# A graph kernel's list writes moved to other places, its boundary tables built earlier, and a skip product spread over a group

## The reference

```python
edge_index = stack([src, dst])
x = layernorm(x + L0(x, edge_index, ...))              # five attention convolutions
x = layernorm(x + L1(x, edge_index, edge_type, W, attn))   # relation layer, 4 relations
x = layernorm(x + L2(x, edge_index, W1, b1, W2, b2))   # two normalised graph convolutions, elu between
x = layernorm(x + L3(x, src, dst, edge_weight, weight, bias))

def conv(x):            # one of L0's five
    q, k, v = x @ Wq + bq, x @ Wk + bk, x @ Wv + bv    # 4 heads of 32
    alpha = sum(q[dst] * k[src], -1) / sqrt(32)
    attn = softmax of alpha over the edges of one destination
    return segment_sum(v[src] * attn, dst) + x @ Ws + bs
    # then h = gelu(layernorm(conv(h))) + h, the fifth only gelu

def L3(x, row, col, val, weight, bias):                # here the roles are swapped:
    out = segment_sum(val * (x @ weight)[col], row)    # it sums by the edge's source
    return leaky(out + bias)
```

## Time and profile before

| | |
|---|---|
| median of 3 runs | 5692.46 us (5691.0 to 5696.89) |
| the profiled execution | 5703.85 us; span from the first to the last instruction 5702.0 us |
| TensorE, matmuls | 64% busy, mean granted clock 0.689 |
| VectorE | 59% busy |
| ScalarE | 27% busy |
| GpSimd | 71% busy, 4168 instructions |
| DMA | 681.11 MB, mean 119 GB/s |

### The profile page before, as it was taken

The page is one execution under the profiler, slowest core; times in us unless marked ns, Lnnn a source line. Parts: engine busy times, 40 slices in busy tenths (PEclk is TensorE's granted clock), DMA queues, the critical chain, the costliest instruction groups (busy, mean ns, idle before and its releaser), DMA issues. The chain is left out here.

```text
span 5702.0 us, 84663 instructions
## 1 busy us (share of the span) xinstructions
PE 3639.0 (64%) x17936; PEld 2902.4 (51%) x17937; DVE 3386.0 (59%) x9194; ACT 1523.1 (27%) x3590; POOL 4073.0 (71%) x4168
## 2 busy tenths in 40 slices
PE   5767767666676756666888857777444444446556
PEld 3556546563565445654666546667333333343334
DVE  7777756665666646665666567777434343436665
ACT  4333324332343323332455522332100010000000
POOL 4477577776777777776777677777677767767775
PEclk6777777777677767776899955555655555557777
DMA  7656266554565275644656443331121121112111
GB/s 240 173 169 188 81 202 185 173 156 125 175 189 170 82 207 170 186 131 145 181 171 181 113 92 72 76 72 38 50 52 53 52 62 52 52 48 57 52 53 51
DMA packets 631577, 681.11 MB, mean 119 GB/s; under 512 B 178674, under 2 KB 512952, under 8 KB 631144
## 3 DMA queue, kind: packets, MB, share of 16 engines
q0 software_dynamic: 166480, 384.69, 24.2%
q1 hardware_dynamic: 464792, 293.16, 17.6%
HBM read 620.51 MB, written 56.89 MB: 119 GB/s over the span
## 5 line engine op out<-in xcount | busy, mean ns | idle before, releaser
L620 POOL DMA_INDIRECT kvconv<-kv_tab,src_all x1664 | 1627.2, 978 | 644.4 <-issue 498.5
L620 POOL DMA_INDIRECT rowsg_<-h_tab,src_all x832 | 789.8, 949 | 287.4 <-issue 252.9
L634 POOL DMA_INDIRECT lst_tab<-pay,ord_now x416 | 429.0, 1031 | 223.5 <-issue 124.6
L620 POOL DMA_INDIRECT rows_r<-rel_tab,idx_r x416 | 417.0, 1002 | 143.2 <-issue 123.4
L620 POOL DMA_INDIRECT rowss_<-h_tab,dst_i_g x416 | 398.3, 957 | 161.7 <-issue 121.9
L620 POOL DMA_INDIRECT kvlast<-kv_tab,src_all x416 | 410.0, 986 | 133.7 <-issue 121.9
L1063 ACT ACTIVATE Sconv<-s8conv 128x512 f32<-128x512 fp8e4 x384 | 240.8, 627 | 396.6 <-PE pA1conv L1021 288.8
L1125 DVE TENSOR_TENSOR msgconv<-kvconv,sm_attEconv 128x512 f32<-128x512 f32 x416 | 285.8, 687 | 84.0 <-PE pA1conv L1021 32.9
L1021 PEld LDWEIGHTS pA0conv<-Sconv,msgconv 128*128 128x128 f32 x1664 | 299.8, 254 | 13.5
L1021 PEld LDWEIGHTS pA1conv<-Sconv,msgconv 128*128 128x128 f32 x1664 | 290.4, 246 | 16.9
L1021 PE MATMUL pA0conv<-Sconv,msgconv 128*128 128x128 f32 x1664 | 298.5, 339 | 0.0
(11 more groups left out here) (655 smaller groups left out, 8961.6 us busy)
## 6 DMA issues: line engine op xcount, KB each, us to landing
qwinconv<-q_tab SPq DMA_DIRECT2D x1664, 64.0 KB
kvconv<-kv_tab,src_all POOLq DMA_INDIRECT x1664
st8conv<-st_tab SPq DMA_DIRECT2D x52, 512.0 KB
s8conv<-s_tab SPq DMA_DIRECT2D x52, 512.0 KB
qwinlast<-q_tab SPq DMA_DIRECT2D x416, 64.0 KB
kv_tab<-stageconv_n SPq DMA_DIRECT2D x28, 512.0 KB
rowsg_<-h_tab,src_all POOLq DMA_INDIRECT x832
q_tab<-stageconv_n SPq DMA_DIRECT2D x28, 256.0 KB
```

The lines of the kernel that those rows point to most:

```text
L620: nc.gpsimd.indirect_dma_start(rows[:, par * TG + t, :], None, tab, bass.IndirectOffsetOnAxis(ap=idx[:, g * TG + t:g * TG + t + 1], axis=0 ...
L634: nc.gpsimd.indirect_dma_start(lst_tab, bass.IndirectOffsetOnAxis(ap=ord_now[:, i:i + 1], axis=0), pay[:, i, :], None).then_inc(sem("liste ...
```

## The change

- **Listings.** The first convolution is treated like the middle ones: 26 listings behind its last gather, 34 in its joint. For that SyncE loads the first 60 tiles of the order in its `conv_edges`, as soon as the order table is stored, no longer at the head of the joint. The relation layer lists 3 tiles after a group instead of 6. Joint n1 lists 12 instead of 22, and joint e1, which had none, lists 20; they are loaded among the loads of layer g1.
- **Border tables.** They are made in `conv_project`: SyncE loads the four rows of tile borders ahead of the weights and the 12 segment pieces behind them, VectorE makes `rowrF` and `rowrB` ahead of its first copy of a projection, and one seventh of the work for `rstF` and `rstB` behind each of the seven blocks.
- **Skip product.** One of the seven products and its copy stand at the end of each of the turns 1 to 7 of group 0, instead of all ahead of the first turn. This holds for the first four convolutions.

```diff
-EACH = 6
+EACH = 3
 BEHIND_REL = 50
-LISTED = [JOINT + (CONVS - 2) * PER, DRAIN + 28, EACH * (GROUPS - 1), BEHIND_REL + 22]
+LISTED = [(CONVS - 1) * PER, DRAIN + 28, EACH * (GROUPS - 1), BEHIND_REL + 12, 20]
...
@@ tables: VectorE
-                        v.memset(rowrF[:, :], NEG)
-                        link(v.memset(rowrB[:, :], NEG))
-                        dve.wait_ge(seg_in, 16 * (3 * H + 4))
-                        v.tensor_copy(edge_f[:, :, :], edge_i[:, :, :])
-                        link(v.tensor_copy(seg_f[:, :, :], seg_i[:, :, :]))
...
@@ tables: SyncE
-                        for h in range(H):
-                            for k, rows in enumerate((dst_row, prev_row, next_row)):
-                                sp.dma_start(seg_i[h * TG:(h + 1) * TG, k, :], rows).then_inc(seg_in, 16)
-                        for k, row in enumerate((first_row, first_next, last_row, last_prev)):
-                            sp.dma_start(edge_i[:, k, :], row.to_broadcast([R, T])).then_inc(seg_in, 16)
...
+        def skip_block(pe, l, b, nx, pc):
+
+            if b == 0:
+                pe.wait_ge(sem("nx_wsc"), l + 1)
+            if b >= 2:
+                pe.wait_ge(sem("nx_skip_out"), l * NB + b - 1)
+            nc.tensor.matmul(pc[b % 2][:, :], nx["wsc"][:, :], xT[:, b * BW:(b + 1) * BW], start=True,
+                             stop=True).then_inc(sem("nx_skip"), 1)
...
@@ conv_project: SyncE
+                    for k, row in enumerate((first_row, first_next, last_row, last_prev)):
+                        sp.dma_start(edge_i[:, k, :], row.to_broadcast([R, T])).then_inc(edge_in, 16)
                     load_next(sp, 0, nx)
+                    for h in range(H):
+                        for k, rows in enumerate((dst_row, prev_row, next_row)):
+                            sp.dma_start(seg_i[h * TG:(h + 1) * TG, k, :], rows).then_inc(seg_in, 16)
                     store_rows(sp, 0, stage)
@@ conv_project: VectorE
+                    made, seg = sem("o_edge"), sem("o_seg")
+                    v.memset(rowrF[:, :], NEG)
+                    v.memset(rowrB[:, :], NEG)
+                    dve.wait_ge(edge_in, 64)
+                    v.tensor_copy(edge_f[:, :, :], edge_i[:, :, :]).then_inc(made, 1)
...
+                    def segments(b):
+                        if b < 3:
+                            if b == 0:
+                                dve.wait_ge(seg_in, 16 * 3 * H)
+                            v.tensor_copy(seg_f[:, b, :], seg_i[:, b, :]).then_inc(seg, 1)
+                        elif b == 3:
+                            dve.wait_ge(seg, 3)
+                            v.tensor_tensor(blocks(rstF[:, :], P), blocks(seg_f[:, 0, :], P), blocks(seg_f[:, 1, :], P),
+                                            ALU.not_equal).then_inc(seg, 1)
...
                     for b in range(NB):
                         stage_block(dve, 0, b, nx, pp, stage)
+                        segments(b)
@@ conv_next: GpSimd and SyncE
-                    list_rows(pool, JOINT, 0 if isinstance(l, int) else MID)
-                    pool.wait_ge(sem("listed"), 16 * PER * l + 16 * JOINT)
+                    list_rows(pool, JOINT, MID)
+                    pool.wait_ge(sem("listed"), 16 * PER * (l + 1))
...
-                    if isinstance(l, int):
-                        order_in(sp, 0, JOINT)
@@ conv_edges: GpSimd
-                    if rank is None:
-                        pool.wait_ge(sem("ord_in"), 32 * (l + 1))
-                        if not isinstance(l, int):
-                            settle(pool)
-                        list_rows(pool, MID if deg is None else DRAIN)
+                    pool.wait_ge(sem("ord_in"), 32 * (l + 1))
+                    if not isinstance(l, int):
+                        settle(pool)
+                    list_rows(pool, MID if deg is None else DRAIN)
@@ conv_edges: SyncE, behind the store of ord_tab
                         sp.wait_ge(sem("k_out"), 16)
+                        order_in(sp, 0, PER)
@@ conv_edges: TensorE, at the end of a turn (ScalarE has keep_skip alike)
+                        if nx is not None and skip(g) and 1 <= q <= NB:
+                            skip_block(pe, l, q - 1, nx, pA)
                     for q in range(RING - 1):
                         scores(0, q, 0)
-                    if nx is not None:
-                        skip_blocks(pe, l, nx, pA)
                     all_turns(pe, turn, OUT)
...
-                        order_in(sp, l * PER - MID, PER)
+                        order_in(sp, l * PER, PER)
@@ norm_joint n1: GpSimd
-                        pool.wait_ge(sem("listed"), 16 * T)
+                        pool.wait_ge(sem("listed"), 16 * sum(LISTED[:4]))
@@ elu_joint
+                @block.gpsimd
+                def _(pool):
+                    list_rows(pool, LISTED[4])
+                    pool.wait_ge(sem("listed"), 16 * T)
@@ last_layers: loads of g1
+                                 (ord_now[:, 0:LISTED[4]], ord_tab[:, T - LISTED[4]:T]),
+                                 (pay[:, 0:LISTED[4], :], edges_c[:, T - LISTED[4]:T, :])],
```

More of the change, by code:

```diff
@@ L705, in stage_block, with keep_skip, blocks @@
                                         ALU.add).then_inc(sem("nx_copied"), 1)
[L707 to L720 removed]
+        def skip_block(pe, l, b, nx, pc):
[5 more added lines that the diff above has]
+                             stop=True).then_inc(sem("nx_skip"), 1)
+        def keep_skip(act, l, b, nx, pc):
+            act.wait_ge(sem("nx_skip"), l * NB + b + 1)
+            nc.scalar.activation(nx["skip"][:, b * BW:(b + 1) * BW], pc[b % 2][:, :], ACT.Identity,
+                                 bias=nx["bsc"][:, :]).then_inc(sem("nx_skip_out"), 1)
         def conv_project(nx, sb, pb):
+            v = nc.vector
             stage = sb("stage", [P, 3, 4, 3 * D])
+            seg_i, seg_f = sb("seg_i", [P, 3, GROUPS * P], i32), sb("seg_f", [P, 3, GROUPS * P])
+            edge_i, edge_f = sb("edge_i", [R, 4, T], i32), sb("edge_f", [R, 4, T])
+            edge_in, seg_in = sem("o_edge_in"), sem("o_seg_in")
+            def blocks(t, n):
+                return t.rearrange("p (g e) -> p g e", e=n)
             pp = [pb(f"pp{i}", [P, 512]) for i in range(3)]
@@ L744, in _ @@
                 def _(dve):
+                    made, seg = sem("o_edge"), sem("o_seg")
[3 more added lines that the diff above has]
+                    v.tensor_copy(edge_f[:, :, :], edge_i[:, :, :]).then_inc(made, 1)
+                    ends = [(o, a, b, h) for o, a, b in ((blocks(rowrF[:, :], ROW), 2, 3),
+                                                         (blocks(rowrB[:, :], ROW)[:, :, ::-1], 0, 1)) for h in range(H)]
+                    at = lambda a, h: slice(h * (TG + 1) + (a == 2), h * (TG + 1) + (a == 2) + TG)
+                    dve.wait_ge(made, 1)
+                    for o, a, b, h in ends:
+                        v.tensor_tensor(o[:, :, at(a, h)], blocks(edge_f[:, a, :], TG),
+                                        blocks(edge_f[:, b, :], TG), ALU.not_equal).then_inc(made, 1)
+                    dve.wait_ge(made, 1 + len(ends))
+                    for o, a, b, h in ends:
+                        v.tensor_scalar(o[:, :, at(a, h)], o[:, :, at(a, h)], NEG, None, ALU.mult)
+                    def segments(b):
[7 more added lines that the diff above has]
+                                            ALU.not_equal).then_inc(seg, 1)
+                        elif b == 4:
+                            v.tensor_tensor(blocks(rstB[:, :], P)[:, :, ::-1], blocks(seg_f[:, 0, :], P),
+                                            blocks(seg_f[:, 2, :], P), ALU.not_equal).then_inc(seg, 1)
+                        else:
+                            dve.wait_ge(seg, b - 1)
+                            o = rstF if b == 5 else rstB
+                            v.tensor_scalar(o[:, :], o[:, :], NEG, None, ALU.mult)
                     dve.wait_ge(sem("nx_w"), 64)
@@ L1101, in turn @@
                             scatter_cast(*far)
+                        if nx is not None and skip(g) and 1 <= q <= NB:
+                            keep_skip(act, l, q - 1, nx, pA)
                         if started(g) and q == 3:
```

36 lines of the change are left out of this document (2 added, 34 removed).

## The result

The changed kernel takes 5671.58 us (median of 5 runs, 5667.21 to 5673.21) where the kernel before took 5692.46 (5 runs, 5691.0 to 5702.89): ratio 0.9957, 95% interval 0.9946 to 0.9969. It is faster, as forecast, but by 21 us of the medians and not by 50, and 5671.58 lies 10.6 us above the upper end of my range. The profiled execution after took 5671.31 us (span 5669.5), right at its median; the one before was 11.4 us over its own. So the traces differ by 32.5 us and the medians by 20.9; when I set stages beside each other, it is the 32.5 that has to come out. On some chips the same kernels run slower (there the kernel before takes 7505 to 7575 us, TensorE's mean granted clock is 0.65 to 0.66 and the engines wait longer for each other), and runs of such a chip are compared only with each other.

The account below looks back on a forecast made before the run. GpSimd, issuing indirect DMAs one after another, was taken to bound the kernel, standing still only at borders. The terms summed to -50.4 us, 5703.85 to 5653.4 profiled, less 11.4 for the median: 5642 us, range 5628 to 5661.

Parts of the forecast that it names:

- Relation layer: Three listings fewer in each of twelve groups, with GpSimd still the pace: 46.1 us off, bounds 46.3 and 34.
- The rival of VectorE's chain: In the relation layer VectorE's chain becomes the pace, half of the 46 us is lost: 5665 us; chance 0.13.
- The tables block: Border-table work leaves this block, GpSimd's 64 gathers then end it at 120.9 against 137.3: 16.0 us off, bounds 13 and 16.5.
- first layer's tail: 26 listings behind the first convolution's last gather end at 693.3, against 685.9: 7.4 us on, bounds 5 and 9.
- The projection block: Border-table work moved in: edges start copies 3.3 us late, segments add, load wait some 0.5 us; 8.0 us on, bounds 5 and 13.
- n1: Joint n1, ten listings fewer, SyncE's stores end it, next block 2.3 us behind: 7.9 us off, bounds 5 and 8.
- e1: Joint e1, 20 listings where GpSimd had none, with 4.7 us for landing and border: 8.3 us on, bounds 5 and 12.
- the rival of the held port: In e1 VectorE's products hold one listing in each of seven blocks, 4.8 us on top: 5647 us; chance 0.10.
- Skip product: First layer's group 0, products spread over the turns: 0.5 us off, nothing in the other layers.
- My sign to look for: If right, the second group's first wait in the first layer is still over 70 us.
- The rival of TensorE's lower clock: In the first layer's group 0 TensorE runs at 1.2 GHz, adding about 9 us: 5651 us; chance 0.08.
- The median: Whole kernel: the runs' median is 11.4 us less than the profiled execution, so 5653.4 becomes 5642.

Follow-up runs that it names:

- each2_b: all_three with 2 listings a group instead of 3 in the relation layer and 22 listings each in n1 and e1; 5648.20 us, ratio 0.9915 to the kernel before.
- tail_wait: The kernel after, with GpSimd waiting in each convolution's tail until its listings have landed; 5679.14 us, ratio 0.9969 to the kernel before.
- tail18_b: The kernel after with 18 listings instead of 26 in the first layer's tail, 42 in its joint; 5673.91 us, ratio 0.9957 (tail18, slower chip: 7455.42 us, 0.9926).
- late_end: gather48 with GpSimd waiting for ScalarE's last copy at the tables block's end; 7480.20 us (kernel before 7574.69); as late_end_c 5658.88 us (kernel before 5710.04).
- tail10: The kernel after with 10 listings in the first layer's tail, 50 in its joint; slower chips: 7529.60 us (kernel before 7574.69), as tail10_b 7491.47 us (7506.75).
- seg_later: The kernel after with each piece of VectorE's segment work one block of copies later in the projection block; 5664.35 us, ratio 0.9942 to the kernel before.
- after_again: The kernel after, unchanged, run again on another call's chip; 5671.25 us, ratio 0.9957 to the kernel before.
- lists_only: The kernel before with only the new places of the listings, without early tables or spread skip products; 5668.20 us, ratio 0.9951 to the kernel before.
- gather48: The kernel after with the last 16 of 64 early gathers moved to the head of the next block; 5659.74 us, ratio 0.9933 to the kernel before.
- all_three: The kernel after with the edits of seg_later and gather48, and 18 listings in n1, 14 in e1; 5647.50 us, ratio 0.9913 to the kernel before.

## Why the prediction was wrong in size

- **Relation layer: right** (-46.1, measured -46.7), bound and all. The rival of VectorE's chain did not come, but it was 0.8 us a group away, as each2_b shows (45.7 us a group against 44.95), not the 1.1 that I had.
- **The tables block is the first failed step.** "Then GpSimd's 64 gathers are last: they end at [...] 120.9, against 137.3": they are last, and end 80.3 us behind the first, but the next block opens 5.5 us behind the last one. I counted the end of GpSimd's last row as the end of the block. Term -16.0, measured -11.5.
- **The same step in the first layer's tail:** "GpSimd ends at 693.3 where today the block ends at 685.9. That is 7.4 us on". GpSimd ended at 692.0, the block at 700.4. +13.8 instead of +7.4, and my bound was 9. The row that should have warned me was in the trace of before: in the tails of the loop's layers, which do list, the next block's first listing stands 9.8 us behind the last one; I had used the 4.7 us of joint n1 for e1 and nothing at all here. tail_wait and tail18_b show the cost, the three late_end runs that ten microseconds of waiting do not hide it, and tail10 that it vanishes where other engines end some 15 us later.
- **The projection block:** "The wait for the segment loads, 2.5 MB that must land by about 22, costs some 0.5 us." It was 5.57, 5.1 us more, of the 5.2 by which the term missed (+13.2 for +8.0). The late start was right (3.2 us, forecast 3.3). The rest of the segment work came to 5.0 us for 4.2, and 2.0 of them are VectorE's waits for a TensorE that had stood, and fell to its lower clock; the border behind is 0.5 shorter. I gave the loads a deadline and did not work out whether the DMA engines could meet it at some 220 GB/s, which the trace of before showed. seg_later takes 5.0 us of it back.
- **n1:** the stores ended the block as forecast, but their last issue came 24.4 us into it and not 22.9, and the next block 3.8 us behind it, not 2.3: 3.1 us mis-sized. **e1:** five of the 20 listings took 1.24 to 1.46 us beside VectorE instead of 0.97, about 2.2 us. That looks like the rival of the held port in a small form, with less than half its price; that it is the port, no run shows.
- **Skip product:** between a loss of 0.2 and a gain of 0.9 us, forecast a gain of 0.5. My sign to look for ("the second group's first wait in the first layer still over 70 us") was wrong by my own sum, which makes that wait shorter by what the tables block gains; it was 63.0.
- **The rival of TensorE's lower clock** had the right engine in the wrong place: the clock fell, but in the projection block, behind the 5.78 us in which TensorE stood for the segment loads.
- **The median.** I took the 11.4 us by which the profiled execution exceeded five runs as fixed. With 17 runs of the kernel before between 5693.5 and 5705.8, it has no ground; on after_again's chip the medians differ by 26.1 us, near the 29.0 of the terms. It also decided where the range lay: without it the range would have been 5639 to 5672, which just holds 5671.58. That would have been luck, for three terms would have been as wrong.

The mechanisms were right but for the border. The projection block, the tables block and the first tail make 5.2 + 4.5 + 6.4 = 16 of the 21 us between -50.4 and -29.0; the last two, 10.9 us, are the border.

## What to carry to other kernels

Where GpSimd with its indirect DMAs ends a stage, the stage costs more than GpSimd's last row: read the distance from GpSimd's last DMA to the next block at a border of the same kernel where GpSimd does come last (here 3 to 9 us), and leave it that much room, or move its last DMAs into the next stage, where 16 of them ran beside other work for nothing. Work that is moved ahead takes its loads with it: divide their bytes by what the DMA engines moved for the same loads before you give them a deadline, and count what an engine that stands meanwhile loses on its clock. And compare a forecast with many runs of the kernel before, not with the offset of one profiled execution.

## What the runs showed of the hardware

- For 7 us behind the last listing's bytes (693.0 to 700.4) no engine works and no DMA moves, and a wait of GpSimd for the landing adds 1.23 us to it. At the border behind the early gathers the closing is 5.5 us, and 4.7 where GpSimd first waits idle for ten. With GpSimd through 15 to 16 us ahead (tail10, tail10_b, tail18) nothing of it is left: TensorE's gap is 1.28 us as in the kernel before.
- The gap belongs to the place in the program, not to chance. From one listing to the next behind the middle tails it is 9.77 or 9.78 us in every kernel of the faster chips but tail_wait; in the first tail it is 9.05 behind 26 listings (after, after_again, lists_only), 8.39 behind 18, and 8.08 behind 26 where 16 gathers stand at the head of the same block (gather48, all_three, each2_b, late_end_c). In e1, where GpSimd also waits for the landing, it is 4.08 behind 22, 3.91 behind 20 and 3.41 behind 14. The number of listings alone doesn't explain it, and what does stays open.
- TensorE stood 5.78 us in the projection block of the kernel after and then ran at a granted clock of 0.66 from 25 to 35 us; in seg_later it stood 2.95 us and stayed at 1.00.
- In the first joint one listing takes 3.49 us at 724.44 (4.31 before), beside a reciprocal of VectorE of 3.33 us that begins at 723.21. The Trainium skill, page "SBUF — State Buffer" (section "SBUF: two separate sides"), says that VectorE can hold the port that GpSimd's descriptors need. The row fits that, though it ends 1.4 us behind the reciprocal, and no run shows that it is the port. And the gathers beside VectorE's table building (66.8 us busy in the 70 us from 53 to 123) take 0.95 us each, as elsewhere, so at any rate not every VectorE instruction delays them.
